# Attention's layer-1 output product from high and low parts: ScalarE makes the high part, VectorE the low part ahead of the router's ranks

## The reference

```
normed = _layer_norm(x, ln_w, ln_b)
k = einsum('btd,ed->bte', normed, Wk);  v = einsum(..., Wv);  r = sigmoid(einsum(..., Wr))
state = DECAY * state + (1 - DECAY) * (k * v)        # scan over time
y = r * states
y = einsum('btd,ed->bte', y, Wo)
return x + y
```

## Time and profile before

| what | us |
|---|---|
| median of three runs | 1149.59 |
| profiled execution | 1149.51 |
| its span, first to last instruction | 1147.2 |
| TensorE busy in the span | 1052.3 |
| VectorE busy | 903.2 |
| GpSimd busy | 657.2 |
| ScalarE busy | 633.2 |
| layer-1 output products in the trace, first and last start | 30.9 and 450.4 |

### The profile page before, as it was taken

How to read it: one execution, slowest core, us unless ns; L and a number is a source line. 1 busy time by engine, 2 the same in 40 slices (tenths; PEclk the granted TensorE clock), 3 DMA queues, 4 the chain that set the end, 5 groups by cost and what they waited for, 6 DMA issues and landing times. The chain is left out here.

```text
span 1147.2 us, 22276 instructions
## 1 busy us (share of the span) xinstructions
PE 1052.3 (92%) x6690; PEld 925.1 (81%) x6690; DVE 903.2 (79%) x1990; ACT 633.2 (55%) x1101; POOL 657.2 (57%) x558
## 2 busy tenths in 40 slices
PE   6999999999999998789999999999999999999900
PEld 5788888787878786568888888888899999999900
DVE  5689998888888898676876677777778788888746
ACT  3455555555555554465454565565656666666528
POOL 2111545454555554565876777677658777777434
PEclk9899999999999999999999999999999999999955
DMA  4011221111121121556656877777778899899469
GB/s 185 19 46 65 56 56 57 56 55 55 55 55 55 55 56 38 179 137 183 134 107 182 193 199 205 186 215 186 217 192 203 241 268 234 241 252 242 83 219 385
DMA packets 81633, 167.74 MB, mean 146 GB/s; under 512 B 28224, under 2 KB 45504, under 8 KB 81312
## 3 DMA queue, kind: packets, MB, share of 16 engines
q1 hardware_dynamic: 51552, 131.41, 36.1%
q0 software_dynamic: 30016, 35.55, 16.6%
HBM read 121.82 MB, written 45.09 MB: 145 GB/s over the span
## 5 line engine op out<-in xcount | busy, mean ns | idle before, releaser
L883 POOL DMA_INDIRECT x_acc<-fy_sb,pair_out x135 | 251.5, 1863 | 115.3 <-issue 41.4
L1430 PE MATMUL ring<-fxh,fw_hi 128*128 128x256 f32 (+1 forms) x720 | 233.8, 325 | 3.6 <-ACT fxh L742 2.2
L1432 PE MATMUL ring<-fxh,fw_lo 128*128 128x256 f32 (+1 forms) x720 | 231.9, 322 | 0.0
L1431 PE MATMUL ring<-fxl,fw_hi 128*128 128x256 f32 (+1 forms) x720 | 231.7, 322 | 0.0
L637 ACT ACTIVATE fw_hi<-w_raw 128x1024 fp32r<-128x1024 f32 x162 | 169.8, 1055 | 78.7 <-PE out L1501 77.6
L969 DVE TENSOR_TENSOR fw_lo<-w_raw,fw_hi 128x1024 fp32r<-128x1024 f32 x162 | 196.6, 1219 | 14.7 <-ACT fw_hi L637 13.9
L103 POOL DMA_INDIRECT xg<-x_src,pair_in x135 | 156.9, 1162 | 67.4 <-issue 48.4
L811 POOL TENSOR_TENSOR rs<-ve,neg_half 128x4 f32<-128x4 f32 x48 | 55.7, 1160 | 225.4 <-DVE nm L920 225.4
L1251 PE MATMUL ring<-xh,w_hi 128*128 128x512 f32 x384 | 162.4, 423 | 3.9 <-issue 3.3
L93 POOL DMA_INDIRECT slot_list<-pairs,slot_u x128 | 133.8, 1046 | 46.7 <-issue 32.4
L1499 PE MATMUL out<-fw_hi,gh 128*128 128x256 f32 x540 | 153.9, 285 | 1.1 <-DVE slot_u L1028 1.1
(11 more groups left out here) (154 smaller groups left out, 1991.5 us busy)
## 6 DMA issues: line engine op xcount, KB each, us to landing
w_raw<-w_ffn SPq DMA_DIRECT2D x162, 512.0 KB, 4.9
x_in<-h SPq DMA_DIRECT2D x16, 512.0 KB, 3.2
x_src<-x SPq DMA_DIRECT2D x16, 512.0 KB, 4.3
x_acc<-x SPq DMA_DIRECT2D x16, 512.0 KB, 5.3
acc<-x_acc SPq DMA_DIRECT2D x16, 512.0 KB, 7.7
out<-o SPq DMA_DIRECT2D x16, 512.0 KB, 6.7
xg<-x_src,pair_in POOLq DMA_INDIRECT x135, 4.8
x_acc<-fy_sb,pair_out POOLq DMA_INDIRECT x135
```

Of the source, the lines that this page charges most:

```text
L883: nc.gpsimd.indirect_dma_start(x_acc, bass.IndirectOffsetOnAxis(pair_out[j][:, q, 0:1].bitcast(U32), 0), fy[j][:, q, :], None, compute_op= ...
L1430: nc.tensor.matmul(out, hi, rows_hi, start=dc == 0, stop=False)
L1431: nc.tensor.matmul(out, hi, rows_lo, start=False, stop=False)
L1432: last = nc.tensor.matmul(out, lo, rows_hi, start=False, stop=dc == DC - 1)
```

## The change

For layer 1 the output product is made of three fp32r products. ScalarE copies Wo of layer 1 to its high part (w_out_hi, in w_out_parts at column 61), and VectorE makes its low part once at the start (low_out). In each of the steps 0 to 15 ScalarE copies y of layer 1 to y_hi, and VectorE subtracts it into y_lo, behind the statistics of z and ahead of choose. Both parts lie in columns of the first expert's weight tiles, fw_hi0 and fw_lo0, which the experts need only later. TensorE waits for y_lo in place of y. Layer 2 keeps its plain product. To make room, the tile pad lies in u, and the second fy tile lies in x1T; add_input of step 1 waits for the first stores of pad and zeros.

```
+OUT_AT = 61
...
-        w_out = sb("w_out", [P, LAYERS, DC, D])
+        w_out = sb("w_out", [P, DC, D])
+        w_out_parts = sb("w_out_parts", [P, 2 * DC * D + 64], F32R)
+        w_out_hi = w_out_parts[:, OUT_AT:OUT_AT + DC * D].rearrange("p (c d) -> p c d", c=DC)
+        w_out_lo = w_out_parts[:, OUT_AT + DC * D:OUT_AT + 2 * DC * D].rearrange("p (c d) -> p c d", c=DC)
...
+        y_hi, y_lo = (part[0][:, PART[2][0]:PART[2][1]].rearrange("p (c t) -> p c t", c=DC) for part in (fw_hi, fw_lo))
...
-            pad = early("pad", [P, SLOTS // P, 2], I32)
+            pad = (u[:, :, :, :].rearrange("p a q d -> p (a q d)")[:, 0:2 * SLOTS // P].bitcast(I32)
+                   .rearrange("p (n c) -> p n c", c=2))
...
-        fy.append(sb("fy_sb1", [P, Q, D]))
+        fy.append(x1T[:, :, :].rearrange("p c t -> p (c t)").rearrange("p (q d) -> p q d", q=Q))
...
             if within(n, 1, CHUNKS):
-                eng.wait_ge(s_po[l], n * 2)
+                if l == 0:
+                    eng.wait_ge(s_y_lo, n)
+                else:
+                    eng.wait_ge(s_po[l], n * 2)
...
+                if layer1:
+                    act.wait_ge(s_y[0], s * 2 + 2)
+                    if within(s, 1, CHUNKS):
+                        act.wait_ge(s_po[0], s * 2)
+                    nc.scalar.activation(y_hi, y[0][:, :, :], ACT.Copy).then_inc(s_y_hi, 1)
                 if within(s, 3, CHUNKS - 1):
                     keep_gates(s)
...
+            def low_out():
+                dve.wait_ge(s_whi[0], DC + 1)
+                nc.vector.tensor_tensor(w_out_lo, w_raw[:, 0, :, 3 * D:4 * D], w_out_hi.bitcast(F32),
+                                        ALU.subtract).then_inc(s_wlo[0], 1)
...
             keep_bias(0)
+            low_out()
...
+                if at(s, 1):
+                    dve.wait_ge(s_padst, 64)
...
                     norm_stats(2, z, s - 2)
+                if layer1:
+                    dve.wait_ge(s_y_hi, s + 1)
+                    nc.vector.tensor_tensor(y_lo, y[0][:, :, :], y_hi.bitcast(F32), ALU.subtract).then_inc(s_y_lo, 1)
...
+                        if l == 0:
+                            hi, lo = (part[:, dc, q * P:(q + 1) * P] for part in (y_hi, y_lo))
+                            nc.tensor.matmul(to, hi, w_out_hi[:, dc, :], start=dc == 0, stop=False)
+                            nc.tensor.matmul(to, hi, w_out_lo[:, dc, :], start=False, stop=False)
+                            last = nc.tensor.matmul(to, lo, w_out_hi[:, dc, :], start=False, stop=dc == DC - 1)
+                        else:
+                            last = nc.tensor.matmul(to, y[1][:, dc, q * P:(q + 1) * P],
+                                                    w_out[:, dc, :], start=dc == 0, stop=dc == DC - 1)
...
-                    pe.wait_ge(s_y[0], s * 2 + 2)
+                    if at(s, 0):
+                        pe.wait_ge(s_wlo[0], DC + 1)
+                    pe.wait_ge(s_y_lo, s + 1)
```

More of the change, by code:

```diff
@@ L329, in attention_and_experts @@
         s_y = [sem("y_ready0"), sem("y_ready1")]
+        s_y_hi, s_y_lo = sem("gated_hi"), sem("gated_lo")
         s_po = [sem("out_product0"), sem("out_product1")]
@@ L465, in first_block @@
                     sp.wait_ge(s_whi[l], DC + 1)
-                    sp.wait_ge(s_wlo[l], DC)
+                    sp.wait_ge(s_wlo[l], DC if l else DC + 1)
                 w_row = sp.value_load(table[0:1, 0, 0:1], min_val=0, max_val=(E - 1) * P)
@@ L560, in split_weights @@
                                          scale=lnp[:, 0, l, dc:dc + 1]).then_inc(s_whi[l], 1)
-                nc.scalar.activation(w_out[:, l, :, :], w_raw[:, l, :, 3 * D:4 * D], ACT.Copy).then_inc(s_whi[l], 1)
+                w_out_copy = w_out[:, :, :] if l else w_out_hi
+                nc.scalar.activation(w_out_copy, w_raw[:, l, :, 3 * D:4 * D], ACT.Copy).then_inc(s_whi[l], 1)
             def normalize(i, src, dst, n, done):
@@ L1258, in output @@
                     q = q0 + i
+                    to = out[:, i * D:(i + 1) * D]
                     for dc in range(DC):
-                        last = nc.tensor.matmul(out[:, i * D:(i + 1) * D], y[l][:, dc, q * P:(q + 1) * P],
-                                                w_out[:, l, dc, :], start=dc == 0, stop=dc == DC - 1)
+                        if l == 0:
[6 more added lines that the diff above has]
+                                                    w_out[:, dc, :], start=dc == 0, stop=dc == DC - 1)
                 if columns[-1] == 1:
```

## The result

The changed kernel takes 1168.94 us in the median of 4 runs, beside 1150.53 us for the kernel before on the same chip. One of the four, 1543.04 us at a mean granted clock of 0.651, was in a slow state and is left out of the ratio; the other three took 1168.06 to 1169.74. The ratio is 1.0159, with a 95% interval of 1.0126 to 1.0192: slower by some 18 us, against 16.6 forecast. The profiled execution took 1168.14 us, its span 1166.3.

A forecast was written before the change was run, and what follows sets the result against it. VectorE's instruction order was taken to bound the attention steps. Terms 12.5 + 0 + 2.8 + 0.5 + 0.8 = 16.6 us on 1149.5 gave 1166 us, range 1153 to 1176 (likeliest case 1161 to 1174).

The forecast's parts named there:

- a ring through VectorE, GpSimd, ScalarE and VectorE: Attention step: the 1.22 us hole before kv ends a chain VectorE starts: statistics, GpSimd rstd, ScalarE normalize and k_sb.
- Steps 3 to 14: Steady attention steps: y_lo lengthens VectorE's order by 1.04 us per step, 12.5 us in all.
- the lower bound, 0.85: Steady steps: 0.85 us each, 10.2 in all, if another 0.2 us is waiting that y_lo covers.
- Step 15: VectorE waits 2.3 us for the gates directly behind y_lo's place, so y_lo costs nothing there.
- Step 0: First attention step: product starts 3.4 us later; VectorE's second residual 1.0 to 3.5 us later, taken as 2.8.
- Steps 1 and 2: Early attention steps: y_lo holds up GpSimd's rstd, 0.5 us and 0.8 us, each between 0 and 1.1.
- Addresses: Tiles moved behind w_out: the same matmuls run alike on different tiles, so 0 us.
- the likeliest case: Whole kernel: VectorE's order bounds the attention steps, so 1166 us, between 1161 and 1174; chance 0.78.
- TensorE as the bound: Rival, attention steps 1 to 15: TensorE's saving of 0.74 us per step decides, 1141 us; chance 0.07.
- The series: Rival, steady steps: VectorE's delay and TensorE's saving on one path, 0.30 us per step, 1157 us; chance 0.06.
- "Absorbed": Rival, steady steps: the 1.22 us hole shrinks to take y_lo, only the beginning is paid, 1154 us; chance 0.06.
- The clock: Rival, steady steps: TensorE's longer waits drop its clock, 12 x 1.7 us more, 1187 us; chance 0.03.

The follow-up runs named there:

- k_sb first: ScalarE's second layer-1 k_sb ahead of layer 2's normalize, steps 2 to 15: kernel before 1144.18 us; rearranged early steps 1144.37; that plus GpSimd y_lo (steps 3 to 15) 1144.24.
- The run with the plain product: Changed kernel with y_hi and y_lo still made and waited for, but layer 1's product in plain 32 bits, low part of Wo left out: 1168.42 us.
- rearranged early steps: Changed kernel with step 0's y_hi and y_lo ahead of layer 2's weights, and y_lo behind layer 2's first scan in steps 1 and 2: 1163.58 us.

## Why the prediction was right, and where its sizes were off

**The bound.** Right for the place that counted: VectorE's order in the second half of the step. y_lo twice cost 1.14 us each, without y_lo the steps were those of before. One sentence of it was too wide, that the hole in front of kv belongs to a ring through VectorE, GpSimd, ScalarE and VectorE. The runs with k_sb first show that the hole was made by ScalarE's order and could be closed.

**Steps 3 to 14: 12.5 us, measured 11.2.** The step that was read for the earlier trace rows came out at 29.06 us, as written. But the steps alternate: the next one was 28.48 us long before (283.86 to 312.34) and is 29.34 now (297.15 to 326.49), 0.86 more. There the gap between the starts of picked and kv shrank from 0.30 to 0.18 us. So a bit of waiting went there that y_lo covers, which is the case of the lower bound, 0.85, in every second step. One period of a loop over pairs is two steps, and both should have been read.

**Step 15, y_hi, the product.** Step 15 costs 0, as forecast. y_lo fills half of the wait, on VectorE in that step:

```profile
458.49 1.22 DVE L1125 TENSOR_TENSOR fw_lo<-y,fw_hi 128x1024 fp32r<-128x1024 f32 x1
460.80 0.19 DVE L1020 COPY g<-out 128x32 f32<-128x32 f32 x1 [1.10 <-PE out L1338]
```

y_hi is hidden. The product takes 3.04 us, not 2.88, since its records follow each other by 0.12 us; this plays no part.

**Step 0: 2.8 us, measured 3.4.** TensorE's product and VectorE's steps around it:

```profile
32.86 1.22 DVE L1125 TENSOR_TENSOR fw_lo<-y,fw_hi 128x1024 fp32r<-128x1024 f32 x1
...
34.44 0.55 PE L1292 MATMUL out<-w_out_parts,fw_hi 128*128 128x256 f32 x1 [4.67 <-DVE fw_lo L1125]
...
39.67 0.69 DVE L1060 TENSOR_TENSOR xr<-out,x_in 128x512 f32<-128x512 f32 x1 [1.59 <-PE out L1294]
```

The product starts 0.2 us behind the forecast and runs for 5.2 us, nearly the slow end (5.4): after 4.67 us of idle time the granted clock is 0.50, the lower of its two levels (1.2 of 2.4 GHz), from 34.4 to 39.0. The value taken lay between the ends, and the upper end was the right one.

**Steps 1 and 2: 1.3 us, measured 3.4.** The mechanism was named, GpSimd held up, but its size was taken at a part of the hold-up, with TensorE catching up on the rest. The Trainium skill, SBUF — State Buffer, section "Who interferes with whom", lets the loser wait for the whole instruction, from which the prediction estimated 1.1 us for each step. The rows come nearer to that and go beyond: GpSimd is held 0.9 us in step 1 and 0.9 + 0.8 in step 2. The latter are nearly all of step 2's 1.77. In step 1 TensorE also lost clock, 0.70 granted from 58.0 to 62.0, after 1.5 busy of 3 us from 55.0. The run with the plain product helps to take the two apart: there rs starts as long behind step 0's second residual (13.9 us) and is held alike, but the clock, 0.66 from 50 to 54, is 1.00 from 58.0 to 62.0. Its rs of step 1 and the transposes that follow:

```profile
53.80 1.92 POOL L827 TENSOR_TENSOR rs<-ve,neg_half 128x4 f32<-128x4 f32 x1 [8.95 <-DVE nm L936]
...
60.29 1.03 PE L1237 MATMUL tp<-ident,normed 128*128 128x128 f32 x8
```

The same transposes in the changed kernel:

```profile
60.30 1.91 PE L1238 MATMUL tp<-ident,normed 128*128 128x128 f32 x8
```

From the start of nb to step 2's residual this run takes 9.55 us (55.79 to 65.34), the kernel before 9.79 (51.24 to 61.03) and the changed kernel 10.55 (55.52 to 66.07). So of step 1's 1.67 us some 0.9 are GpSimd's hold-up and 0.8 lie behind it, in the stretch with the lower clock. TensorE, which was to catch up on a part, lost time instead.

**Addresses and handover: 0, measured 1.1.** The experts' first matmul starts at 507.1 after 487.2, 19.9 us later; 0.8 of it comes back by the end. GpSimd's first gather of tokens for it (xg) already starts 19.0 us later (495.97 for 476.99), and the 8 transposes of these tokens take 1.97 us for 1.09, with a granted clock of 0.65 from 504 to 508. No run tried the cause. And from step 16's residual to the end of the span, the profiled executions of all the kernels here take 695.7 to 701.2 us, so 1.1 us between two of them says little.

**The sum.** 19.1 us of span against 16.6 stayed inside the likeliest case (1161 to 1174). In part the errors cancel: 1.3 us too much in steps 3 to 14 stand against 3.8 too little in the other terms.

**The rivals.** TensorE as the bound is refuted for the changed kernel by the plain product, and for the kernel before by the run without y_lo, whose steps are no shorter with the shorter product; it is true only with k_sb first. The series would have made the plain product cost more, which it did not. "Absorbed" failed because y_lo lies behind the hole; work in front of it, as u, is absorbed. The clock stayed at 1.00 in the steady steps; before the experts it fell in steps 0 and 1 and, in both kernels, behind step 16's residual (0.58 from 472 to 476 us; 0.63 there in the kernel before).

## What to carry to other kernels

On an engine that works in order, ask of each place whether a wait follows it before the next meeting point: work in front of a wait is free up to the wait's length, and taking it away gains nothing; work behind it costs its whole length. Here taking u away from in front of a wait gained nothing, y_lo in front of step 15's wait cost nothing, and behind the waits it cost 1.1 us a step. Ask next what makes the wait: here a ready instruction stood behind another's wait on a third engine, and moving it by one place gained 6.5 us in the kernel before and 19 in the changed one with rearranged early steps. A fuller engine becomes the bound only once such a hole is closed, so a saving on it has to be tried again then.

## What the runs showed of the hardware

A subtraction of 128x1024 takes 2.40 us on GpSimd and 1.22 on VectorE. While GpSimd ran an addition of that size (u, 2.40 us), VectorE's product of two tiles in SBUF took 2.86 us in place of 0.68, ending 0.55 us after GpSimd's record (264.98 to 265.53); statistics kept their time. Unexpected was ve, a TENSOR_SCALAR of 128x4 with one tile read: 0.50 us in place of 0.17, ending with GpSimd's y_lo (280.13 and 280.11). The Trainium skill, SBUF — State Buffer, section "Who interferes with whom", counts tensor_scalar among the operations that can, under conditions, take the port pair shared with GpSimd; these rows agree.
